# Layer 1 of a CIN tower: pairs made on TensorE and squared on ScalarE, against pairs multiplied on VectorE out of rows that come back from DRAM

## The reference, cut to what matters

```python
# B, M, D = 1024, 39, 16; S1 = S2 = 128; everything float32
def cin_layer(x0, xk, W, b):
    out = einsum('bhd,bmd,shm->bsd', xk, x0, W) + b[None, :, None]
    return relu(out)
e  = stack([tbl_f[ids[:, f]] for f in range(39)], axis=1)      # B x 39 x 16
x1 = cin_layer(e, e, W1, b1)          # layer 1: all pairs of the 39 fields
x2 = cin_layer(e, x1, W2, b2)         # layer 2: 128 channels x 39 fields
z  = concatenate([x1.sum(-1), x2.sum(-1)], axis=-1)
h  = relu(concatenate([z, dense_ctx]) @ W_top1 + b_top1)
y  = relu(h @ W_top2 + b_top2) @ W_top3
```

## Time and profile before

| | |
|---|---|
| median of 3 executions | 1174.59 us (1174.16 to 1176.11) |
| profiled execution: time, span | 1172.96 us, 1171.2 us |
| TensorE, VectorE busy | 1137.7 us (97%), 1068.0 us (91%) |
| GpSimd, ScalarE busy | 895.7 us (76%), 688.0 us (59%) |
| mean granted TensorE clock | 0.985 |

### The profile page before, as it was taken

The page is one execution under the profiler, slowest core; times in us unless marked ns, Lnnn a source line. Parts: engine busy times, 40 slices in busy tenths (PEclk is TensorE's granted clock), DMA queues, the critical chain, the costliest instruction groups (busy, mean ns, idle before and its releaser), DMA issues.

```text
span 1171.2 us, 19309 instructions
## 1 busy us (share of the span) xinstructions
PE 1137.7 (97%) x4942; PEld 907.8 (78%) x4942; DVE 1068.0 (91%) x3821; ACT 688.0 (59%) x2167; POOL 895.7 (76%) x930
## 2 busy tenths in 40 slices
PE   4699999999999999999999999999999999999998
PEld 2377777888887888888888777888888888888876
DVE  4268889999999999999999888999999999999976
ACT  3365555666665666666666556666766666667542
POOL 6388989888888888889889767888887546555542
PEclk9599999999999999999999999999999999999998
DMA  6101111111111111111111110111111000000000
GB/s 200 6 3 7 7 7 7 7 7 7 8 7 7 8 7 6 8 7 7 7 7 7 6 6 4 7 7 7 8 7 6 1 1 1 1 1 1 1 1 1
DMA packets 170381, 12.00 MB, mean 10 GB/s; under 512 B 163630, under 2 KB 169262, under 8 KB 170141
## 3 DMA queue, kind: packets, MB, share of 16 engines
q1 hardware_dynamic: 160029, 8.13, 7.8%
q0 software_dynamic: 10240, 2.64, 2.9%
HBM read 8.31 MB, written 0.00 MB: 7 GB/s over the span
## 4 chain that ended last, share of the span: by engine, by line
PE 93%; DVE 3%; issue 2%; POOL 1%; ACT 1%; DMA 0%; POOLq 0%; SPq 0%; ACTq 0%; DVEq 0%
PE ps L941 24%; PE ps L942 24%; PE ps L945 24%; PE ps L895 4%; PE ps L913 3%; PE ps L908 3%; PE ps L909 3%; PE ps L911 3%; PE ps L975 3%; DVE acc L823 2%; PE ps L883 1%; POOL looked L449 1%; PE ps L952 1%; PE ps L902 1%; PE ps L1031 0%
## 5 line engine op out<-in xcount | busy, mean ns | idle before, releaser
L823 DVE SCALAR_TENSOR_TENSOR acc<-ps,e,acc 128x128 f32<-128x128 f32 x3186 | 852.4, 344 | 42.1 <-PE ps L945 30.5
L941 PE MATMUL ps<-w2h,x1h 128*128 128x512 f32 (+1 forms) x1280 | 514.7, 402 | 2.4 <-DVE acc L823 0.9
L458 POOL TENSOR_TENSOR fy<-fy 128x512 f32<-128x512 f32 (+1 forms) x256 | 402.6, 1573 | 145.8 <-ACT fy L583 131.3
L942 PE MATMUL ps<-w2l,x1h 128*128 128x512 f32 (+1 forms) x1280 | 495.6, 387 | 0.0
L945 PE MATMUL ps<-w2h,x1l 128*128 128x512 f32 (+1 forms) x1280 | 493.8, 386 | 0.0
L583 ACT ACTIVATE fy<-ps,e 128x128 f32<-128x128 f32 x1536 | 415.7, 389 | 65.0 <-PE ps L945 61.7
L449 POOL DMA_INDIRECT looked<-in_table,rows x320 | 307.6, 961 | 68.6 <-issue 37.0
L941 PEld LDWEIGHTS ps<-w2h,x1h 128*128 128x128 f32 x1280 | 241.5, 189 | 65.2 <-DVE acc L823 7.9
L942 PEld LDWEIGHTS ps<-w2l,x1h 128*128 128x128 f32 x1280 | 241.1, 188 | 51.7 <-issue 7.6
L945 PEld LDWEIGHTS ps<-w2h,x1l 128*128 128x128 f32 x1280 | 240.8, 188 | 48.7 <-DVE x1l L769 0.7
L615 ACT ACTIVATE zh<-ps 128x512 fp32r<-128x512 f32 x156 | 96.3, 617 | 177.6 <-PE ps L895 173.9
(11 more groups left out here) (93 smaller groups left out, 660.5 us busy)
## 6 DMA issues: line engine op xcount, KB each, us to landing
e<-looked SPq DMA_DIRECT2D x360, 5.0 KB, 1.9
looked<-in_table,rows POOLq DMA_INDIRECT x320
e<-looked SPq DMA_DIRECT2D x120, 4.5 KB, 1.9
w_st<-in_w SPq DMA_DIRECT2D x1, 1728.0 KB
wt_sb<-in_wt SPq DMA_DIRECT2D x2, 512.0 KB
w_st<-in_w SPq DMA_DIRECT2D x1, 768.0 KB, 6.0
w_sb<-in_w1a SPq DMA_DIRECT2D x1, 448.0 KB
w1b_sb<-in_w1b SPq DMA_DIRECT2D x1, 448.0 KB
```

What stands on the lines that cost most here:

```text
L458: nc.gpsimd.tensor_tensor(out, a, b, ALU.add).then_inc(s_fsum, 1)
L823: nc.vector.scalar_tensor_tensor(acc[:, sub, :] if m < fields("D", last)[-1] else y, y, emb(p, sub, m), acc[:, sub, :] if m else fsum[:, p ...
L941: nc.tensor.matmul(y, x1h[:, t % 2, at], w2h[:, cols], start=True, stop=False)
L942: nc.tensor.matmul(y, x1h[:, t % 2, at], w2l[:, cols], start=False, stop=False)
```

## The change

Layer 1's pairs are no longer made on TensorE. SyncE writes a tile's looked-up rows to DRAM (`keep_fields`, `fields_d`, field by position, the first 20 fields a second time below the 39), reads them back for `e` (`by_position`), and reads each of the six chunks of 128 pairs back as two 128x512 arrays, first factors and second factors (`fetch`, four or five transfers a chunk, 2 KB a row, into `ab`). VectorE multiplies the two in SBUF (`product`, L404, fp32, in place; `POOL_CHUNKS` is empty, so none is on GpSimd), and one fp32 matmul a chunk takes the product (L893), for all tiles. Twelve pairs are still multiplied directly, and go through DRAM instead of the transposes (`keep_pairs`, `by_pair`, `to_pass`). The expansions, the squares, `zl`, the split weights of layer 1 and the transposes are gone. The columns of layer 1 now stand in another order, so ScalarE (x1h, x1) and VectorE (`x1l`, now L782) read the accumulator with a step of 4 or 16 numbers. A product stands six slots ahead of its matmul (`AHEAD`), three for tile 2. Lookups are 11 instead of 12 a tile from pair 4 on, and one more tile is looked up ahead of the loop.

```diff
+POOL_CHUNKS = ()
+AHEAD, AHEAD_FIRST = 6, 3
+SECOND_PRODUCTS = {0: (0,), 1: (1,), 2: (2,), 3: (3,), 4: (4, 5)}
+ACT_FETCHES = (3, 4, 5)
+LAYER1_AT = (6, 9, 11, 14, 16, 19, 21)
+LAYER1_SECOND = (9, 11, 13, 15, 17, 19, 21)
...
 def lookups(p):
-    return 6 if p == 0 or p >= 4 else 5
+    return 6 - p % 2
...
+        def product(engine, t, v):
+            engine.wait_ge(s_ab[v], 16 * len(segments(v)) * (t + 1))
+            engine.tensor_tensor(ab[:, v, 0, :], ab[:, v, 0, :], ab[:, v, 1, :], ALU.mult).then_inc(
+                s_z_pool if by_pool(t, v) else s_z_dve, 1)
+        def fetch(engine, t, v):
+            engine.wait_ge(s_kept[t], 3 * 16)
+            if t:
+                engine.wait_ge(s_mm1, C1 * (t - 1) + v + 1)
+            for row, count, h, shift in segments(v):
+                first = (t * X_ROWS + h) * N
+                engine.dma_start(ab[row:row + count, v, :, :], bass.AP(fields_d.tensor, first, [[N, count], [shift * N, 2], [1, N]])
+                                 ).then_inc(s_ab[v], 16)
...
+                for t in range(2, TILES):
+                    for v in range(C1):
+                        if v == 0 and t > 2:
+                            keep_pairs(t - 1)
+                        fetch(sp, t, v)
+                        if v == 1 and t > 2:
+                            by_pair(t - 1)
+                        if v == 3 and t + 1 < TILES:
+                            keep_fields(t + 1)
+                        if v == 4 and t + 1 < TILES:
+                            by_position(t + 1)
...
-                nc.scalar.activation(zh[:, k % 2, :], src, ACT.Square).then_inc(s_z1, 1)
-                nc.scalar.activation(src, src, ACT.Square).then_inc(s_sq, 1)
...
-                    nc.vector.tensor_tensor(zl[:, k % 2, :], ps[:, BK_T, :], zh[:, k % 2, :], ALU.subtract).then_inc(s_zl, 1)
...
+                    x, high, low = (ps[:, BK_ACC1, :].rearrange("s (k g) -> s g k", g=DT),
+                                    *(y[:, t % 2, :].rearrange("s (g k) -> s g k", g=DT) for y in (x1h, x1l)))
+                    nc.vector.scalar_tensor_tensor(low, x, 0.0, high, ALU.max, ALU.subtract).then_inc(s_x1l, 1)
...
-                        nc.tensor.matmul(ps[:, BK_ACC1, :], w1h[:, v, :], zh[:, k % 2, :], start=False, stop=False)
-                        nc.tensor.matmul(ps[:, BK_ACC1, :], w1l[:, v, :], zh[:, k % 2, :], start=False, stop=False)
-                        mm = nc.tensor.matmul(ps[:, BK_ACC1, :], w1h[:, v, :], zl[:, k % 2, :], start=False, stop=(v == C1 - 1))
+                    nc.tensor.matmul(ps[:, BK_ACC1, :], w1_sb[:, v, :], ab[:, v, 0, :], start=(v == 0), stop=False).then_inc(s_mm1, 1)
```

More of the change, by code:

```diff
@@ L35, with segments @@
 LOOKED = 8
-HELD = 4
-SOON = 6
 SHIFTS = (M + 1) // 2
-ZP = 15
+ZP = 12
 K1 = P
-C1 = -(-(SHIFTS * M - ZP) // K1)
-SPLIT = (0, 1, 2, 3, 4, 5)
-ZH, ZW, ZL = 2 * M, 96, 112
-ONE_H, ONE_L = ZH + ZP, ZW + ZP
+FULL = K1 // M
+C1 = (SHIFTS * M - ZP) // K1
+REST = [(C1 * FULL + k // M, k % M) for k in range(C1 * (K1 - FULL * M))]
+ZH0, ZM0 = M - ZP, SHIFTS - 1 - ZP
+assert REST[-1] == (SHIFTS - 1, ZH0 - 1) and C1 * K1 + ZP == SHIFTS * M
+ZG = ZP + 1
+ZROWS = 3 * ZG
+TWICE = 20
+X_ROWS = M + TWICE
+def segments(v):
+    runs = [(M * k, M, 0, FULL * v + k) for k in range(FULL)]
+    row, n = M * FULL, K1 - M * FULL
+    for shift, pairs in itertools.groupby(REST[n * v:n * (v + 1)], key=lambda pair: pair[0]):
+        pairs = list(pairs)
+        runs.append((row, len(pairs), pairs[0][1], shift))
+        row += len(pairs)
+    return runs
 MB = 4
@@ new lines, in layer1_steps, with by_pool, products_made, products_after @@
+def layer1_steps(p, s):
+    return layer1_slot(SLOTS * p + s)
+def by_pool(t, v):
+    return t > FIRST_TILES and v in POOL_CHUNKS
+def products_made(t, v):
+    mine = by_pool(t, v)
+    return sum(by_pool(u, w) == mine for u in range(t + 1) for w in range(C1) if (u, w) <= (t, v))
+def products_after(p, j):
+    slots = [s for s, kind in enumerate(ORDER) if kind == "D"] + [SLOTS]
+    steps = [(1, v) for v in SECOND_PRODUCTS.get(j, ())] if p == 0 else []
+    for ahead, tiles in ((AHEAD_FIRST, (2,)), (AHEAD, range(3, TILES))):
+        steps += [at for s in range(slots[j], slots[j + 1]) for at in layer1_slot(SLOTS * p + s + ahead) if at[0] in tiles]
+    return [(t, v) for t, v in steps if v < C1 and not by_pool(t, v)]
@@ L197, with pool_products, z_step @@
+def pool_products(p):
+    return [(t, v) for s in range(1, SLOTS + 1) for t, v in layer1_slot(SLOTS * (p + 1) + s) if v < C1 and by_pool(t, v)]
+SPLIT_IN = {2 * t - 4: t for t in range(FIRST_TILES, TILES)}
+HIGH_SLOT = 2
+def z_step(p, s):
+    at = {4: 1} if p == 0 else {}
+    at.update({4: t} if (t := SPLIT_IN.get(p - 1)) is not None else {})
+    return at.get(s)
 CALM = 4
 def lookups(p):
-    return 6 if p == 0 or p >= 4 else 5
-def high_slots(p):
-    return (6, 7) if p == 0 else (4, 5) if p == 2 else (1, 4) if SPLIT_IN[p] < SOON else (3, 6)
+    return 6 - p % 2
@@ new lines, in _ @@
+                by_position(1)
+                for v in range(C1):
+                    fetch(sp, 1, v)
+                keep_pairs(1)
+                keep_fields(2)
+                by_pair(1)
+                by_position(2)
+                for t in range(2, TILES):
+                    for v in range(C1):
+                        if v == 0 and t > 2:
[7 more added lines that the diff above has]
+                            by_position(t + 1)
+                        if t == 2 and v == 5:
+                            for dst, src in mlp_weights:
+                                sp.dma_start(dst, src).then_inc(s_mlpw, 16)
@@ L439, in _ @@
+                keep_pairs(TILES - 1)
+                by_pair(TILES - 1)
                 sp.wait_ge(s_tail, 7)
@@ L549, in _ @@
                     look_ahead(1)
-                    if mine_soon and p != 2:
+                    if mine is not None:
                         low_parts(nc.gpsimd, mine)
@@ L565, in _ @@
                     look_ahead(1)
-                    if mine is not None and not mine_soon:
-                        low_parts(nc.gpsimd, mine)
+                    for at in pool_products(p):
+                        product(nc.gpsimd, *at)
+                    if (soon := SPLIT_IN.get(p + 1)) is not None:
+                        multiplied_out(nc.gpsimd, soon)
                     if p + 2 < PAIRS:
@@ L1041, in pair_rows @@
 def pair_rows():
-    n = np.arange(C1 * K1).reshape(C1, K1)
-    n = n + ZP * (n >= (SHIFTS - 1) * M)
-    shift, h = n // M, n % M
-    return h, (h + shift) % M, shift, shift < SHIFTS
-def selection():
-    sel = np.zeros((2 * M, C1, K1), np.float32)
-    h, m, _, there = pair_rows()
-    for p in range(K1):
-        for k in range(C1):
-            if there[k, p]:
-                sel[[h[k, p], m[k, p]], k, p] = 1
-    sel[M:] = sel[:M]
-    return sel
+    h, m = np.zeros((2, K1, C1), np.int64)
+    for v in range(C1):
+        for row, count, first, shift in segments(v):
+            h[row:row + count, v] = np.arange(first, first + count)
+            m[row:row + count, v] = (h[row:row + count, v] + shift) % M
+    return h, m
 def kernel(**inputs):
```

411 lines of the change are left out of this document (146 added, 265 removed).

## The result

The changed kernel takes 1287.3 us (median of 4 runs, 1283.81 to 1292.9) where the kernel before takes 1174.38 (4 runs, 1172.96 to 1176.11): 1.0964 times as long, 95% interval 1.0927 to 1.1002. The forecast was 1197 us, in a range of 1150 to 1240. The sign was right; 90 us were not foreseen.

A forecast was written before the change was run, and what follows sets the result against it. VectorE and TensorE were taken as nearly tied, TensorE slightly ahead. Afterwards VectorE's 33.15 us plus 1.7 of waits a tile gave +28.7 us with the dense stage, the start -5: 1172.96 + 23.7 = 1197 us, range 1150 to 1240.

The forecast's parts named there:

- the step on the transfers: DMA per tile: factors 10 us, small packets at 9 ns, together 18 us of 35, hidden behind buffers free 24 us ahead.
- The start: Up to layer 2's beginning and the first tiles: lookups through DRAM and back, -5 us in all, between -10 and +8.
- VectorE's waits: Six SBUF products a tile wait for GpSimd's additions: 0.28 us each at random times, 1.7 us a tile.
- The 28.7 us for 29 periods: Tile 2 to tile 31: 29 x 34.85 us, plus 1.8 and 10.6, makes 1023.0 instead of 994.3.
- the 33.15 of an engine that never stands: VectorE's work per tile by instruction count, unchanged by the edit: 33.15 us, before 1.7 us of waits.
- the dense network's first stage: Three tiles where TensorE's matmuls stand: TensorE needs 115.2 us, VectorE 104.6, so 10.6 us come on top.
- The rival of late transfers: Small packets at 53 ns make products late and VectorE wait: half-way 1240 to 1350 us, fully over 1600; chance 0.10.
- the likeliest case: Random to unlucky waits of VectorE's products for GpSimd's additions: 1178 to 1240 us, chance 0.60.
- `x1l` out of PSUM with a step: VectorE's once-a-tile row reading PSUM four numbers apart: between nothing and a doubling of 0.53 us, taken as nothing.
- draining rows keep their pace: VectorE's rows with one operand in PSUM stay 0.258 us apart, undisturbed by GpSimd.
- TensorE is no longer the bound: TensorE's need falls from 33.5 to 32.7 us a tile, so it stops being the bound.
- the slow `x1l` on top of 1231: Rival: additions met at their beginning, 3 us a tile, 1231 us; with a slow `x1l` too, 1240; no separate chance.

The follow-up runs named there:

- z_read16: Changed kernel with the direct pairs' 16-byte pieces moved from the DRAM write to the read back: 1233.51 us, 1.0497 times the kernel before.
- z_late: Changed kernel with only ScalarE's step to_pass moved from slot 4 to slot 9 of its pair: 1244.91 us, 1.0783 times the kernel before.

## Why the prediction was wrong, step by step

**What failed** is the step on the transfers: "Together 18 us of 35, hidden". It failed in its price and in its conclusion. The price: small packets at 9 ns, that of before's packets from SBUF to SBUF, where a 16-byte piece cost 14 ns when read from DRAM and 36 when written there (16 and 44 with what it did to the packets beside it). "The same size of packet" was the wrong likeness; with the pieces on the read side 54 to 81 us came back. The conclusion: a transfer that is hidden was judged by the fetches' buffers, free 24 us ahead, and those were indeed hidden. The direct pairs have a chain of their own, write, wait, read, wait, and ScalarE's step stands at a fixed slot behind it. The prediction did not count the microseconds from the low part to that slot. The sum: 1063.9 us from tile 2 to 31, and 1032.3 with only the step moved, so **31.6 us** of the 69.6. The two were measured on different chips. z_read16, on a chip where before takes the time that it took beside the changed kernel (1174.62 and 1174.38), gives 1063.9 - 1029.1 = 34.8 for the same term, and on the third chip the same difference was 70.2.

**The start**, forecast at -5 between -10 and +8, was +37.9. Of it 13.9 us are the small writes (tile 2 at 148.62, and at 134.71 in z_read16, whose chip ran before in the same time). Some 5 are the weights in front. Most of what is left is the fetches: with half of their bytes, tile 2 came 15.5 us earlier than with the later weights alone, on the second chip. The step counted 10 to 13 us for the factors of tile 0 and gave tiles 1 and 2 "some microseconds"; it took a rate measured in the first 10 us as one that is to be had for three tiles in a row, with small packets between.

**VectorE's waits**, 1.7 us a tile by random meetings, were the right mechanism, and two thirds of the size. The mean of L404 was forecast at 0.97 us and is 0.894, longest 2.93 (forecast: up to 2.9). The 28.7 us for 29 periods measure 1029.1 - 994.3 = **34.8 us** in z_read16, where the round trip costs the periods nothing. That these are close is in part luck. The products of these periods took 33 us more than undisturbed ones, 1.1 a tile, where 1.7 x 29 = 49 were forecast. Two other terms made up for it: the period without these waits is 34.1 - 0.4 = 33.7 us, and not the 33.15 of an engine that never stands, and the three tiles with the dense network's first stage took 118.2 us, and not 115.2. Nor are the waits even: 34.1 us in most tiles as long as lookups stand between the additions, 37.7 after them. "The places are not random" was written there; their pattern decides between 34.1 and 37.8, and one slot's shift made it 37.0 everywhere. The Trainium skill, "SBUF — State Buffer", section "Who interferes with whom", has the rule that a VectorE instruction with two inputs in SBUF contends with a GpSimd one that reads SBUF, and one with at most one does not: the 162 products from PSUM at 670 to 690 ns and the 156 `zl` rows before and after the operand moved agree with it from both sides.

**The rival of late transfers** had the right price, 1240 to 1350, and the wrong victim: "products, not GpSimd, keep VectorE waiting". The products waited 24 us in all. It had been given a chance of 0.10 on the strength of the 9 ns. The Trainium skill, "DMA: Bandwidth & Descriptors", section "Specifications", which names 512 bytes as the smallest transfer at full rate and a read-modify-write below, was cited against the likeliest case and then given no weight, for want of a row. That written pieces of 16 bytes are dear, at 36 ns, is of the sign that it says. But the same kernel also writes 60,416 pieces of 64 bytes to DRAM (`fields_d`), eight times below that size, and these took 11.5 ns on average, median 11. So being small and being written is not enough, and that the mechanism is that one is not shown; size, direction and the order of the addresses were not varied apart.

**Right:** `x1l` out of PSUM with a step costs nothing (median 680 ns); draining rows keep their pace (407.84 - 403.70 = 4.14 us for sixteen, as the earlier trace rows):

```profile
403.70 4.22 DVE L838 SCALAR_TENSOR_TENSOR acc<-ps,e,acc 128x128 f32<-128x128 f32 x16
407.84 0.81 DVE L404 TENSOR_TENSOR ab<-ab 128x512 f32<-128x512 f32 x1
```

TensorE is no longer the bound. **Small misses:** behind tile 31, +3.2 us for the forecast nothing; layer 2 at 56.73, not before 50; the pieces of 64 bytes are 1,888 a tile, not 1,872; by the prediction's own sum the slow `x1l` on top of 1231 gives 1244, not 1240.

The account of the 110.7 us of span: start 37.9; ScalarE's stands 31.6; VectorE's waits and what goes with them 1032.3 - 994.3 = 38.0, of which the products' rows show 33 in z_read16 and 36 in z_late, and the rest isn't followed; the end 3.2. The second and third term rest on z_late, from another chip.

## What to carry to other kernels

When a value goes out to memory and back, follow its own chain to the slot of the instruction that waits for it, with the packets' price from a row of the same size and direction, and ask what is queued behind that instruction; a buffer that is free in time says nothing about it, and moving the waiting instruction five slots gave back as much of the period as making the writes cheap. When two engines that lock each other out are paced by the same banks, a random mean gives the size of the loss but not its value: lay the new places beside the other engine's long rows in every phase of the program, and try a slot to either side.

## What was not expected of the hardware

By the packets' own times in the traces, a 16-byte piece took 7.5 ns on average from SBUF to SBUF, 14 ns read back from DRAM in z_read16 and 36 ns written to DRAM in the changed kernel. The median was 7 to 9 in all three. The writes are dear by a minority: 9% of them took over 100 ns, and in the stretch of writes shown above the core moved 9 GB/s, where its mean is 95. A row of 2 KB took 127 ns on average in z_read16, so one write of 16 bytes costs more than a quarter of 2 KB. One write of 64 bytes took 11.5 ns, a third of what the quarter of its bytes took. Where the dear ones come from isn't known: four neighbouring pieces of 16 bytes share 64 bytes of DRAM and come from four partitions, but nothing here tried that.

The same product row cost between 0.67 and 2.93 us depending on when GpSimd's addition had begun, and the pattern stayed for tens of tiles: 34.1, 37.0 or 37.7 us a tile with the same work.

The kernel before took 1154.22 us on one chip and 1172.89 to 1174.62 on two others; the mean granted clock was 0.996 on the fast one, and 0.983 to 0.989 on the two others. Where in the kernel that clock was lost wasn't followed.
